# Four-block transformer on one core: first weights as a load of their own, value tables cleared by GpSimd, the first norm ahead of the modulation's sums, and PSUM split 7 to 1

## The reference

```
L0: x += g_msa * selfattn(rope(qkv(mod(ln(x)))), 512 x 512 mask) @ W_o
    x += g_x * crossattn(mod(ln(x)), 77 context tokens, mask) @ W_co
    x += g_mlp * (gelu(mod(ln(x)) @ W1 + b1) @ W2 + b2)
L1: nx = ln(x); evidence = softmax(nx Wq (ctx Wk)^T / sqrt(128)) @ (ctx Wv)
    combined = [nx, evidence, anchor]; routed = sum of 3 experts, each weighted by the router
    x += sigmoid(gate(combined)) * (routed @ out_w + out_b)
L2: x += crossattn(ada_ln(x), ada_ln(ctx)) @ Wp + bp
L3: x += g_a * selfattn(mod(ln(x))); x += crossattn(ln(x), ln(ctx)); x += g_m * mlp(mod(ln(x)))
```

## Time and profile before

| | |
|---|---|
| runs, median (lowest to highest) | 981.49 us (980.85 to 984.12) |
| profiled execution | 981.84 us, span 980.0 us |
| TensorE busy | 919.4 us, 94% |
| VectorE busy | 707.8 us, 72% |
| ScalarE busy | 559.4 us, 57% |
| GpSimd busy | 145.1 us, 15% |
| mean granted TensorE clock | 0.97 |

### The profile page before, as it was taken

How to read it: one execution, slowest core, us unless ns; L and a number is a source line. 1 busy time by engine, 2 the same in 40 slices (tenths; PEclk the granted TensorE clock), 3 DMA queues, 4 the chain that set the end, 5 groups by cost and what they waited for, 6 DMA issues and landing times.

```text
span 980.0 us, 15448 instructions
## 1 busy us (share of the span) xinstructions
PE 919.4 (94%) x4986; PEld 397.1 (41%) x4986; DVE 707.8 (72%) x1933; ACT 559.4 (57%) x1036; POOL 145.1 (15%) x388
## 2 busy tenths in 40 slices
PE   3958999999999999999999999998999999999998
PEld 3622434433434444454444443333334333334443
DVE  5688898788888857552454556797988899886742
ACT  5023555664655667674437362574667677676673
POOL 1013000302011121110111120001212111022210
PEclk9777999999999999999999998998999999999999
DMA  8040320222011121100202033012032204014201
GB/s 310 33 129 2 85 61 26 67 77 74 16 55 50 58 78 35 34 7 1 65 4 63 7 115 85 7 65 67 23 115 76 65 2 123 15 34 105 68 14 33
DMA packets 66323, 57.49 MB, mean 59 GB/s; under 512 B 19407, under 2 KB 63427, under 8 KB 65988
## 3 DMA queue, kind: packets, MB, share of 16 engines
q1 hardware_dynamic: 64996, 54.73, 19.5%
q10 hardware_dynamic: 1248, 1.77, 0.5%
HBM read 31.01 MB, written 24.49 MB: 57 GB/s over the span
## 4 chain that ended last, share of the span: by engine, by line
PE 84%; DVE 6%; ACT 3%; issue 3%; DMA 2%; SPq 1%; POOL 0%; ACTq 0%; DVEq 0%; POOLq 0%
PE pv_bank L1540 16%; PE bank L1495 12%; PE bank L1518 11%; PE bank L1520 6%; PE bank L1522 4%; PE bank L1599 3%; PE bank L1646 3%; PE bank L1633 3%; PE bank L1651 3%; PE bank L1600 3%; PE bank L1498 2%; PE bank L1506 2%; PE bank L1565 2%; PE bank L1548 2%; PE bank L1468 2%
## 5 line engine op out<-in xcount | busy, mean ns | idle before, releaser
L1019 ACT ACTIVATE pr<-bank 128x512 f32<-128x512 f32 (+1 forms) x704 | 378.5, 598 | 194.8 <-PE bank L1520 103.0
L1271 DVE CUSTOM_DVE_ANT_0 bank<-bank,mask_q 128x512 f32<-128x512 f32 x256 | 171.3, 709 | 25.6 <-PE bank L1495 24.1
L1495 PE MATMUL bank<-ks,qs 97*128 97x512 bf16 x512 | 178.1, 391 | 12.2 <-issue 6.6
L1274 DVE TENSOR_REDUCE mx<-bank 128x1 f32<-128x512 f32 x256 | 163.4, 683 | 31.5 <-PE bank L1495 30.4
L1518 PE MATMUL bank<-qs,ks 103*128 103x512 bf16 x512 | 181.3, 385 | 1.3 <-DVE mx L1271 0.5
L1540 PE MATMUL pv_bank<-pr,va 128*32 128x512 f32 x1024 | 137.5, 608 | 1.1 <-ACT pr L1019 1.1
L1276 DVE TENSOR_REDUCE mx<-bank 128x4 f32<-128x308 f32 x192 | 83.7, 470 | 26.0 <-PE bank L1498 24.6
L1495 PEld LDWEIGHTS bank<-ks,qs 97*128 97x128 bf16 x512 | 43.9, 98 | 135.1 <-ACT pr L1019 28.1
L1520 PE MATMUL bank<-mask_k,identb 128*128 128x512 bf16 x256 | 98.1, 383 | 0.0
L915 POOL CAST mp<-mx 128x16 bf16<-128x16 f32 x80 | 16.0, 200 | 511.0 <-DVE mx L1271 203.0
L1518 PEld LDWEIGHTS bank<-qs,ks 103*128 103x128 bf16 x512 | 49.6, 98 | 71.8 <-ACT pr L1019 8.9
(11 more groups left out here) (219 smaller groups left out, 1197.6 us busy)
## 6 DMA issues: line engine op xcount, KB each, us to landing
qs<-q_parts SPq DMA_DIRECT2D x40, 384.0 KB, 4.6
q_parts<-xn SPq DMA_DIRECT2D x20, 384.0 KB, 2.6
ks<-k_parts SPq DMA_DIRECT2D x64, 96.0 KB, 3.7
q_parts<-xn SPq DMA_DIRECT2D x20, 256.0 KB, 2.2
k_parts<-u SPq DMA_DIRECT2D x8, 384.0 KB, 2.4
q_parts<-u SPq DMA_DIRECT2D x20, 128.0 KB, 2.1
qs<-mrow SPq DMA_DIRECT2D x160, 6.0 KB
late<-late_w SPq DMA_DIRECT2D x1, 2432.0 KB, 13.6
```

Source lines behind the costliest of these rows:

```text
L1019: act.activation(pr[0:K, 4 * (group % NSLOT) + t % 4, :], bank(k)[0:K, :], ACT.Exp, scale=SCALE).then_inc(act_done, 1)
L1271: dve.tensor_tensor_reduce(b[:, :], b[:, :], mask_q[:, qb, :], 1.0, -3e38, ALU.add, ALU.max, dst[:, qb, g, e:e + 1]).then_inc(dve_done, 1)
L1274: dve.tensor_reduce(dst[:, qb, g, e:e + 1], b[:, :], AX.X, ALU.max).then_inc(dve_done, 1)
L1495: ins = pe.matmul(b[:, :], qs[s][0:R, g, qb * P:(qb + 1) * P], ks[s][0:R, e, g, :], start=True, stop=True)
```

## The change

It does five things, and nothing of the computation is added or dropped: TensorE has 3824 instructions in both programs' lists.

1. The early weights are two transfers: `first_w` (565 columns: vectors, identity, the first block's query, key and value weights) goes second in SP's list, then x of lane 1, then `early_w` (the other 1676 columns) with a semaphore of its own. The steps that read the latter (gates, bias_rows, ctx_k, ctx_v) wait for it.
2. The four `vac` tables are cleared by GpSimd, as a step values_init of the second block, and no longer by DVE in the first. ACT's part of ctx_v waits for it.
3. In the planner each part of mods comes behind a piece of lane 0's first norm on DVE: part 0 behind ln_stats, part 1 behind ln_norm.
4. Seven common PSUM banks and one for pv, in place of six and two; up to three max tiles are planned ahead in place of two.
5. New numbers in `EAGER`, `URGE`, `FAIR`, `CAP`, `TABLE_KEPT` and the loads' assumed landings, so that every engine's list has another order.

```diff
+FIRST_W = (("cols", 32), ("mod_b", NMOD), ("ident", P), ("tail", 2), ("w_qkv0", 3 * D))
+EARLY_W = (("e_b2", E), ("w_rt", 3 * E), ("w_o0", D), ("w_co", D), ("w_p2", D), ("w_pr3", D), ("w_cp3", D), ("w_ck", D), ("w_k1", D),
...
-BANKS, MAX_BANKS, EXP_BANKS, PV_BANKS = 6, 2, 3, 2
-TABLE_LOAD, TABLE_KEPT = 1.3, -130.721
+BANKS, MAX_BANKS, EXP_BANKS, PV_BANKS = 7, 3, 3, 1
+TABLE_LOAD, TABLE_KEPT = 1.3, -139.4644
...
-EAGER = {"chain": 0.4005, "rows": 0.2561, "max": 0.1002, "exp": 0.0224, "pv": -0.1116, "tables": 0.2095}
+EAGER = {"chain": 0.400361, "rows": 0.090382, "max": 0.018103, "exp": 0.04245, "pv": -0.085163, "tables": 10.14809}
...
         if kind == "mods":
-            return [("sp", ("w_ada", "w_mod")[rest[0]])], []
+            return [("sp", ("w_ada", "w_mod")[rest[0]]), ("dve", (0, ("ln_stats", "ln_norm")[rest[0]], 0))], []
...
+        if kind == "ctx_v":
+            return [me("act", "ctx_t")], [("pool", (1, "values_init"))]
...
                 x_load(0)
-                sp.dma_start(early[:, :], io["early_w"]).then_inc(loaded, 16)
-                for s in range(1, LANES):
+                sp.dma_start(early[:, 0:sf], io["first_w"]).then_inc(loaded, 16)
+                x_load(1)
+                sp.dma_start(early[:, sf:], io["early_w"]).then_inc(loaded_early, 16)
+                for s in range(2, LANES):
                     x_load(s)
...
-                for s in range(B):
-                    do(dve.memset(vac[s][:, :, :, :, :], 0.0))
-                    for par in range(2):
-                        dve.memset(vac[s][0:NK, :, :, :, 32 * par + 8:32 * par + 16], 1.0)
...
+                def values_init(k, s):
+                    for o in range(B):
+                        link(pool, pool_link, n, pool.memset(vac[o][:, :, :, :, :], 0.0))
+                        for par in range(2):
+                            ins = pool.memset(vac[o][0:NK, :, :, :, 32 * par + 8:32 * par + 16], 1.0)
+                        if o < B - 1:
+                            link(pool, pool_link, n, ins)
+                    ins.then_inc(pool_done, 1)
```

More of the change, by code:

```diff
@@ L192, in tables @@
 def tables():
-    return of(1, ("mods", 0), ("mods", 1), ("mask_q",), ("keys_init", 0), ("keys_init", 1), ("keys_init", 2), *[("mask_t", kb) for kb in range(TB)], ("bias_rows",), ("anchors_",),
+    return of(1, ("mods", 0), ("mods", 1), ("mask_q",), ("keys_init", 0), ("keys_init", 1), ("keys_init", 2), ("values_init",), *[("mask_t", kb) for kb in range(TB)], ("bias_rows",), ("anchors_",),
               ("e2_t", 0), ("e2_t", 1), ("e2_out", 0), ("e2_out", 1), ("e2_out", 2)) + [("give", "gates")]
@@ L222 @@
 LANDED = {"load": 2.5, "store": 2.2, "part1_out": 2.4, "parts_out": 2.4, "stack": ((4.3, 4.6), (3.,) * HG), "ctx_out": 2.7, "ctx_stack": 2.5, "max_rows": 1.9}
-LOADED = {"w_ada": 0., "w_mod": 3., "trig": 4., "mask": 6., "setup": 9., "late": 13.}
+LOADED = {"w_ada": 0., "w_mod": 3., "trig": 5., "mask": 7., "setup": 11., "late": 16.}
 LINK = {"pe": .35, "act": .22, "dve": .2, "pool": .15, "sp": 0.}
 TABLE = {"exp": 1, "l1_exp": 1, "router_exp": 1, "gate": 1, "expert_h": 2, "gate_h": 2, "mlp_h": 3}
-BANKS, MAX_BANKS, EXP_BANKS, PV_BANKS = 6, 2, 3, 2
-TABLE_LOAD, TABLE_KEPT = 1.3, -130.721
+BANKS, MAX_BANKS, EXP_BANKS, PV_BANKS = 7, 3, 3, 1
+TABLE_LOAD, TABLE_KEPT = 1.3, -139.4644
 RUN_OF = {("mlp_h", 0): True, ("mlp_h", FC - 1): False, ("gate_h", None): True, ("expert_h", 2 * E - 1): False}
-EAGER = {"chain": 0.4005, "rows": 0.2561, "max": 0.1002, "exp": 0.0224, "pv": -0.1116, "tables": 0.2095}
-URGE = ((0.635, 0.099, -0.344, -0.066, 0.264, 0.027, -0.328, -2.376),
[3 rows of a table removed]
+EAGER = {"chain": 0.400361, "rows": 0.090382, "max": 0.018103, "exp": 0.04245, "pv": -0.085163, "tables": 10.14809}
+URGE = ((1.28977, 0.73298, 0.17683, -0.05101, 0.68431, 0.19666, -0.49743, -1.71396),
[3 rows of a table added]
 CLOSING, CORE_PHASE = ("attn_out", "mlp_add", "l1_add"), {0: 0, 1: 1, 2: 4, 3: 5, 4: 6}
-FAIR, CAP = 0.00245, 63.2916
+FAIR, CAP = 0.0025152, 64.20125
 class Order:
@@ L358, in before @@
         simple = {"e2_out": ("dve", "e2_t", 0 if rest == (0,) else 1),
-                  "gates": ("dve", "gate_cols", *rest), "ctx_k": ("act", "ctx_t"), "ctx_v": ("act", "ctx_t"),
+                  "gates": ("dve", "gate_cols", *rest), "ctx_k": ("act", "ctx_t"),
                   "ctx_split": ("dve", "ctx_k"), "ctx_out": ("dve", "ctx_split"),
@@ L585, in column @@
                 at += n
-        early = sb("early", [P, columns(EARLY_W)]); late = sb("late", [P, columns(LATE_W)])
+        early = sb("early", [P, columns(FIRST_W + EARLY_W)]); late = sb("late", [P, columns(LATE_W)])
         def w(name):
-            for held, table in ((early, EARLY_W), (late, LATE_W)):
+            for held, table in ((early, FIRST_W + EARLY_W), (late, LATE_W)):
                 if name in [other for other, _ in table]:
@@ L670, in build @@
         scratch = pr[:, :, :].rearrange("p a n -> p (a n)")
-        sa, sm, sw = columns(SETUP_A), columns(SETUP_A + SETUP_M), columns(SETUP_W)
+        sf, sa, sm, sw = columns(FIRST_W), columns(SETUP_A), columns(SETUP_A + SETUP_M), columns(SETUP_W)
         def setup_w(name):
@@ L964, in ctx_v @@
                 def ctx_v(k, s):
+                    act.wait_ge(pool_done, count("pool", (1, "values_init")))
                     act.wait_ge(pe_done, count("pe", k))
@@ L1129, in gates @@
                 def gates(k, s, l):
+                    dve.wait_ge(loaded_early, 16)
                     dve.wait_ge(pe_done, count("pe", k))
@@ L1436, in ctx_k @@
                     b = free_bank(pe, k)
+                    pe.wait_ge(loaded_early, 16)
                     pe.wait_ge(act_done, count("act", (s, "ctx_t")))
@@ L1714, in layout @@
     arrays["bias_rows"] = np.stack([L2("bp"), L3("b_proj"), L3("b_cproj"), L1("out_b")])
-    for name, table in (("setup_a", SETUP_A), ("setup_m", SETUP_M), ("setup_o", SETUP_O), ("setup_e", SETUP_E), ("early_w", EARLY_W), ("late_w", LATE_W)):
+    for name, table in (("first_w", FIRST_W), ("setup_a", SETUP_A), ("setup_m", SETUP_M), ("setup_o", SETUP_O), ("setup_e", SETUP_E), ("early_w", EARLY_W), ("late_w", LATE_W)):
         arrays[name] = np.concatenate([parts[part] for part, _ in table], axis=1)
```

10 lines of the change are left out of this document (5 added, 5 removed), and 6 rows, old and new, of the table URGE.

## The result

The changed kernel takes 975.18 us (median of 7 runs, 972.65 to 979.2), the kernel before 980.89 us beside it: a ratio of 0.9944, 95% interval 0.9922 to 0.9966. That is 5.7 us faster, and it lies outside the 0.3% that count as no change. The direction and the range held; the size did not: 14.5 us were forecast. The profiled run took 974.82 us, its span is 973.0 us (before: 981.84 and 980.0).

The account below looks back on a forecast made before the run. TensorE, 84% of the chain, was taken as the bound, with waits for PSUM banks and a slow beginning. From 981.84 us, 0 - 12.4 - 2.2 + 0.6 - 1.0 = -15.0 gave 966.8, as median 966.5 us; range 956 to 981 us.

Parts of the forecast that it names:

- The start: Up to the second block's barrier: TensorE's first product at 10.7 us, 1.6 us earlier, with SP's last issue just ahead.
- The rival of a short issue: SP's long setup issue goes too: 4.4 us earlier at the barrier, about 960 us; chance 0.12.
- The beginning, 0 us: First norm and tables up to the first max tile, still at about 62.4 us: 0, ends -3.9 and +2 us.
- The seventh bank, -12.4 us between 600 and 900: 113 weight-load waits each one 0.22 us step shorter, 24.9 us at most, half taken.
- the first rival: Seventh bank buys nothing, as TensorE's waits are for DVE's and ACT's pace: 980 to 982 us; chance 0.12.
- The seventh bank elsewhere, -2.2 and nothing: 100 to 370 us: half of 20 waits by 0.22 us, -2.2 us; nothing for the rest.
- One values bank, +0.6: At 39 handovers between halves, 18 steps in the median hide ACT's copy; one exposed copy taken, +0.6 us.
- GpSimd's clearing: Clearing beside the sums costs nothing; as a rival it holds DVE, +4 us on the tables, 970.5 us, chance 0.05.
- The new order, -1.0 for table loads: ACT loads function tables 18 times against 21: -1.0 us (0 to -3.8); the other reordering left unpriced.

Follow-up runs that it names:

- quick readers: Changed kernel with DVE's maxima and ACT's exponentials of the second self attention cut to half the columns: 971.13 us; the same on six common banks and one for values: 978.72 us.

## Why the prediction was wrong, by its steps

- **The start.** Right: TensorE at 10.36 us for 10.7, SP's last issue at 9.40 us just ahead, setup_o's issue 3.02 us and its neighbour's 1.23, 4.25 us together (before: 4.42 and 0.43). The rival of a short issue is out.
- **The beginning, 0 us.** The first max tile came at 63.11 us for 62.4, so the number held, but by luck: two errors cancel. The tables took 18.5 us instead of 13.6, the four rotated products 3.7 us instead of 7.2: I took each duration from where it stood before, and both had been set by the clock of the moment. At the first exponential the beginning costs 1.4 us in the two profiled executions, less than the 2 us by which executions differ there.
- **The seventh bank, -12.4 us between 600 and 900.** This is the step that failed, "113 x 0.22 = 24.9 us at most ... I take half". It measured 4.3 us there by the milestones, some 7 us if both executions had had one clock (an estimate, above). A half was too much at both ends of the chain of reasoning: of 15.6 us of waits that went, 5.5 came back in other loads, and of the 10.1 us left only 4.3 reached the end. The reason may be that a weight load's wait can lie behind a product that is still running; no run measured this. That the waits were wholly for the readers' pace (the first rival) is wrong too: the bank is worth something, with quick readers as well.
- **The seventh bank elsewhere, -2.2 and nothing.** 0.9 us as far as 365 us, 2.1 us from there to 589 us, where I had excluded it, and 1.3 us in the tail, each from one execution on either side. In all 9.2 us by the ratios, where 14.6 were forecast.
- **One values bank, +0.6.** Right within what can be measured: two are no faster (1.1 us slower, with 3 us of uncertainty). TensorE's waits there in the changed kernel:

```profile
PE pv_bank L1556 <- ACT pr L1031: 0.8, 3, 0.3
```

- **GpSimd's clearing.** It did hold DVE (below), and it cost nothing: TensorE had its sums until 18.6 us, and its pause from there to the tables is 2.71 us with either clearing.
- **The new order, -1.0 for table loads.** This is the other step that failed: "The rest of the reordering has no row that prices it", and so it was put at nothing. The run on six and two banks priced it. The new order and the new start together are 4.8 us slower there than the kernel before (2.3 to 7.4), where the prediction's terms for both make them 1.0 us faster. Which part of the order loses them was not found; the table loads were not priced by themselves.

By the ratios the change adds up as +4.8 us for the order and the start, -1.1 for giving up a values bank and -9.2 for the seventh common bank, -5.5 in all. The prediction had -1.0, +0.6 and -14.6. So the order's term misses by 5.8 us and the bank's by 5.4 us, both towards a smaller gain.

## What to carry to other kernels

A wait that a view names is not yet time: of the waits that a buffer takes away, count what comes back at the next wait, and then what lay behind running work, before any of it goes into a sum; here 15.6 us of named waits were worth 4.3, or some 7 at one clock. The price of one more buffer falls steeply with their number (40, then 9 us), so it can't be taken by count times step. A new order has a price of its own, which shows when it is run on the old buffers, and two executions are compared at one clock before a few microseconds are read from their difference. And a duration read in one place holds in another only if TensorE's clock is the same there.

## What the runs showed of the hardware that was not expected

TensorE ran at half speed where the granted clock's column shows full speed. From 22 to 34 us of the changed kernel the window says 1.00:

```profile
22.00:34.00 12.00, 12.00 (x53) 10.54 (x50) 2.21 (x5) 0.16 (x1) 0.00 (x0) 1.00 0.04 9
```

Yet the fourteen products at 27.28 us took 3.15 us there and 1.73 us in the kernel before, both after TensorE had been through the 8.24 us of sums and a pause. That is 0.225 us each against 0.124; of the two levels, 1.2 and 2.4 GHz, the durations say the lower one. The 38 products of the sums, of the same shape, took 8.24 us in both kernels, 0.217 us each, and there too the column says 1.00. The Trainium skill, TensorE: Matmul & The Clock Gate, "What's actually happening", has the lower level as the default that activity lifts; the rows agree in so far as the slow stretch follows a pause (2.71 us before the tables) and ends while TensorE is kept busy (the rotated products at 42.33 us take 1.02 us, 1.91 us in the kernel before at 46.52 us). Its "Seeing it yourself" warns that recorded clock events can be unreliable, and this window bears that out.

GpSimd's clearing shut DVE out for about one of its own instructions. Timeline of the changed kernel, and below it the kernel with DVE's clearing:

```profile
14.37 1.06 POOL L893 MEMSET vac<- 128x1152 f32 x1
...
14.60 0.86 DVE L1113 TENSOR_SCALAR affine<-mod,early 128x4 f32<-128x4 f32 x1
```

```profile
16.54 0.23 DVE L1107 TENSOR_SCALAR affine<-mod,early 128x4 f32<-128x4 f32 x1
```

DVE's four columns ended at 15.46 us, just behind the clearing's 15.43. This agrees with the Trainium skill, SBUF — State Buffer, "Who interferes with whom", by which a DVE tensor_scalar in a two-port mode is blocked for the whole length of a GpSimd instruction that was issued first; the profile does not show the mode. The time shows nothing of it, since nobody was waiting.
